# Qkv stage in steps of 256 rows, the first ones beside chunks 10 to 15 of the convolution

## The reference

```python
K = 2.0 * einsum('chn,hnl->chl', C_term, V).real        # 16 images, 256 channels, 64 states -> 256 positions
h = K
h = h + attn(_layernorm(h))    # layer_norm, qkv, elu(q)+1, elu(k)+1, kv = sum k v, ksum = sum k,
                               # (q kv) / (q ksum), proj, residual, layer_norm, fc1, gelu, fc2, residual
h = h + ffn(_layernorm(h))     # sigmoid(x Wq routers^T), 256 leaf probabilities, leaf values, Wout
```

## Time and profile before

| | us |
|---|---|
| median of 3 runs | 537.11 |
| the profiled execution | 535.44 |
| its span | 533.6 |
| PE busy in the span | 444.3 (83%) |
| DVE, ScalarE, GpSimd busy | 357.8, 286.7, 184.6 |
| chain of waits: PE, DVE, issue, ScalarE, GpSimd | 60%, 18%, 8%, 7%, 4% |

### The profile page before, as it was taken

The page is one execution under the profiler, slowest core; times in us unless marked ns, Lnnn a source line. Parts: engine busy times, 40 slices in busy tenths (PEclk is TensorE's granted clock), DMA queues, the critical chain, the costliest instruction groups (busy, mean ns, idle before and its releaser), DMA issues.

```text
span 533.6 us, 11354 instructions
## 1 busy us (share of the span) xinstructions
PE 444.3 (83%) x3724; PEld 401.4 (75%) x3724; DVE 357.8 (67%) x854; ACT 286.7 (54%) x592; POOL 184.6 (35%) x166
## 2 busy tenths in 40 slices
PE   0076666668999997799999999999999999998983
PEld 0066655556777776698998998998988988998973
DVE  5999999666778655254657567567566576485764
ACT  3814554457766673545754654555466366446621
POOL 0597998130211111051810811612504406306020
PEclk9997999899999999699999999999999999999988
DMA  4624657711111221000101101002002001001011
GB/s 120 209 86 110 162 157 222 211 54 72 41 41 59 102 67 41 25 16 0 41 2 40 40 0 58 20 0 79 0 0 79 0 0 39 0 0 39 1 41 39
DMA packets 37817, 30.86 MB, mean 58 GB/s; under 512 B 19488, under 2 KB 31136, under 8 KB 37792
## 3 DMA queue, kind: packets, MB, share of 16 engines
q1 hardware_dynamic: 18688, 22.04, 12.9%
q10 hardware_dynamic: 19104, 8.52, 5.6%
HBM read 17.97 MB, written 12.58 MB: 57 GB/s over the span
## 4 chain that ended last, share of the span: by engine, by line
PE 60%; DVE 18%; issue 8%; ACT 7%; POOL 4%; DVEq 1%; DMA 1%; ACTq 0%; SPq 0%; POOLq 0%
PE PS L297 17%; PE PS L299 16%; PE PS L298 16%; PE PS L1458 6%; DVE Mb L988 3%; PE PS L1587 3%; DVE M L991 3%; PE PS L1513 2%; DVE lTl L1193 1%; DVE outb L1253 1%; ACT PS L628 1%; DVE bst L1199 1%; ACT yh L632 1%; ACT kr L660 1%; ACT lTh L740 1%
## 5 line engine op out<-in xcount | busy, mean ns | idle before, releaser
L1222 DVE TENSOR_TENSOR gl<-PS,gh 128x512 fp32r<-128x512 f32 x56 | 38.7, 691 | 65.6 <-ACT gh L748 37.2
L745 ACT ACTIVATE PS<-PS,fc1bias 128x512 f32<-128x512 f32 x56 | 36.7, 656 | 76.6 <-PE PS L299 76.6
L297 PE MATMUL PS<-fc2h,gh 128*128 128x256 f32 x256 | 74.4, 291 | 2.4 <-DVE gl L1349 1.4
L299 PE MATMUL PS<-fc2l,gh 128*128 128x256 f32 x256 | 72.4, 283 | 0.0
L298 PE MATMUL PS<-fc2h,gl 128*128 128x256 f32 x256 | 72.3, 283 | 0.0
L489 POOL TENSOR_SCALAR pst<-mv 128x4 f32<-128x4 f32 x15 | 3.4, 228 | 181.7 <-DVE pst L1206 181.7
L297 PE MATMUL PS<-x2Th,fc1h 128*128 (+2 forms) x144 | 55.3, 384 | 2.1 <-DVE x2Tl L1193 2.1
L298 PE MATMUL PS<-x2Th,fc1l 128*128 (+2 forms) x144 | 53.7, 373 | 0.0
L299 PE MATMUL PS<-x2Tl,fc1h 128*128 (+2 forms) x144 | 53.3, 370 | 0.0
L297 PEld LDWEIGHTS PS<-fc2h,gh 128*128 128x128 f32 x256 | 48.7, 190 | 5.8 <-DVE pst L1206 1.6
L298 PEld LDWEIGHTS PS<-fc2h,gl 128*128 128x128 f32 x256 | 48.8, 191 | 1.2
(11 more groups left out here) (229 smaller groups left out, 1366.0 us busy)
## 6 DMA issues: line engine op xcount, KB each, us to landing
h_scratch<-tokev ACTq DMA_DIRECT2D x16, 256.0 KB, 3.1
h<-h_scratch SPq DMA_DIRECT2D x16, 256.0 KB, 4.9
q_scratch<-qe ACTq DMA_DIRECT2D x16, 256.0 KB, 2.1
qf<-q_scratch SPq DMA_DIRECT2D x16, 256.0 KB, 3.0
out_tokens<-outb SPq DMA_DIRECT2D x16, 256.0 KB, 2.1
craw<-in_c_ri SPq DMA_DIRECT2D x16, 128.0 KB, 2.6
craw<-in_c_ri SPq DMA_DIRECT2D x32, 64.0 KB, 2.3
fc1raw<-in_fc1T SPq DMA_DIRECT2D x1, 1024.0 KB, 6.2
```

Of the source, the lines that this page charges most:

```text
L297: pe.matmul(dst, ah, bh, start=start, stop=False, **kw)
L299: return pe.matmul(dst, ah, bl, start=False, stop=stop, **kw)
L745: act.activation(bank(j % 2), bank(j % 2), ACT.Gelu, bias=fc1bias[:, j:j + 1]).then_inc(gact, 1)
L1222: dve.tensor_tensor(gl[:, j % 2, :], bank(j % 2), gh[:, j % 2, :].bitcast(F32), ALU.subtract).then_inc(gldone, 1)
```

## The change

The qkv stage becomes 16 steps of 256 rows: step s is half `s // 8` of images 2(s mod 8) and 2(s mod 8)+1. As steps 0 to 7 need only the first half of `h0`, `scales`, `norm1`, q, k and v of steps 0 to 3 are made in the same rounds as chunks 12 to 15, and the preparation of step 0 and 1 in the rounds of chunks 10 and 11. In these rounds one PSUM bank (0) takes the tokens of all chunks and one (7) the table; PE's `tokens` waits for the copy of the chunk before. The k/v of steps 0 to 7 stay in SBUF (k in `kvm`, v in `vt0`). For images 0 to 7 the sums of both halves are made together in the second pass (4 matmuls); for images 8 to 15 the first half is summed and masked in steps 4 to 8 (`kv_sums_ahead`), the second half later into `kvx`, and GpSimd adds the two (`add_halves`, 8 times 128x272). SyncE's queue now also sends the token rows of chunks 10 to 15 and all of q. The set-up operations on projection, gate, leaf, fc1 and fc2 weights are moved between the steps 4 to 10. Attention of images 0 and 1 stands behind step 12, projection behind step 14.

The core of the diff (numbers of lines are not kept):

```diff
+STEPS = 2 * GROUPS
+FIRST = 12
+SINGLE = 10
+SPREAD = STEPS - 4
+AHEAD = GROUPS
...
+            load_h0(0)
+            load_h0(1)
+            load_h0(2)
+            load_c(FIRST // 2, FIRST % 2)
+            store_h0(SINGLE)
+            for n in range(SINGLE + 1, CHUNKS):
+                if n + 2 < CHUNKS:
+                    load_c((n + 2) // 2, (n + 2) % 2)
+                load_h0(n - SINGLE + 2)
+                if n > FIRST:
+                    store_q(n - FIRST - 1)
+                store_h0(n)
...
+            rotate(SINGLE // 2, 0)
+            for n in range(SINGLE, CHUNKS):
+                if n + 1 < CHUNKS:
+                    rotate((n + 1) // 2, (n + 1) % 2)
+                scales(n - FIRST + 2)
+            for s in range(CHUNKS - FIRST + 2, STEPS):
+                scales(s)
...
+            add_proj_bias(0)
+            for c in range(AHEAD, AHEAD + 4):
+                add_halves(c)
+            rstd(0, x2done, 11, mv2, pst2, xh2done, 4, v2done)
+            for c in range(AHEAD + 4, B):
+                add_halves(c)
...
+            for n in range(SINGLE, CHUNKS):
+                s = n - FIRST
+                if s + 1 >= 0:
+                    norm1_apply(s + 1)
+                products(n, 7)
+                if s >= 0:
+                    q_elu(s)
+                product_sums(n, n % 2)
+                norm1_stats(s + 2)
...
+                if s + 1 >= 0:
+                    y_low(s + 1)
+                if s >= 0:
+                    k_elu(s, 0)
+                    k_elu(s, 1)
+
+            def step(s):
+                if s + 1 < STEPS:
+                    norm1_apply(s + 1)
+                q_elu(s)
+                if s > GROUPS:
+                    kv_mask(image(s - 1, 0))
+                elif image(s - 1, 0) >= AHEAD:
+                    kv_mask_ahead(image(s - 1, 0))
+                if s + 1 < STEPS:
+                    y_low(s + 1)
+                k_elu(s, 0)
+                if s + 2 < STEPS:
+                    norm1_stats(s + 2)
...
+                k_elu(s, 1)
...
+            for n in range(SINGLE, CHUNKS):
+                s = n - FIRST
...
+                if s >= 0:
+                    q_products(s)
+                if s + 1 >= 0:
+                    y_transposes(s + 1)
+                if s >= 0:
+                    kv_products(s, 0)
+                    kv_products(s, 1)
+                pe.wait_ge(tokout, CREDIT + (n if n > SINGLE else n - 1))
+                tokens(n, n % 2, 0)
+
+            def step(s):
+                q_products(s)
...
+                if s + 1 < STEPS:
+                    y_transposes(s + 1)
+                kv_products(s, 0)
...
+                kv_products(s, 1)
```

More of the change, by code:

```diff
@@ L346, in _ @@
                 load_weight(dst[:, :, :], src)
-            for n in range(2, CHUNKS):
+            for n in range(2, FIRST):
                 load_c(n // 2, n % 2)
@@ L735, in high @@
+            step(GROUPS + 3)
             def high(dst, b, made, g, used, uses, done):
@@ L1096, in kv_mask, with tile @@
-            def kv_mask(u, i):
-                c = 2 * u + i
-                dve.wait_ge(ksmm, CREDIT + (3 + i if u == 0 else 2 * (c + 1)))
-                new = PS[:, 6 if u >= EARLY else 6 + i, 0:KD * (P + 1)].rearrange("p (k x) -> p k x", k=KD)
-                m = kvm[:, c, :, :]
+            for n in range(CHUNKS // 2, SINGLE):
+                products(n, 7 - n % 2)
+                product_sums(n, n % 2)
+            def tile(s, i):
+                return h0[:, s // GROUPS, image(s, i), :]
@@ L1159, in _ @@
+            step(CHUNKS - FIRST + 2)
+            step(CHUNKS - FIRST + 3)
+            dve.wait_ge(act_set, 5)
+            for j in range(2):
+                w = slice(j * JH // 2, (j + 1) * JH // 2)
+                tt(fc2l[:, w, :], fc2raw[:, w, :], fc2h[:, w, :].bitcast(F32), ALU.subtract)
+                step(GROUPS + j)
+            for k in range(KD):
+                dve.wait_ge(act_set, 6 + k)
                 link(dve.scalar_tensor_tensor(fc1l[:, k, :], fc1raw[:, k, :], nrm[:, 2, k:k + 1],
@@ L1494, in kv_products @@
[L1494 to L1500 removed]
+                        mm = three(pe, PS[:, 5, o * HT:(o + 1) * HT], qkvh[:, k, w], qkvl[:, k, w], yh[:, s % 2, k, :],
+                                   yl[:, s % 2, k, :], k == 0, k == KD - 1)
@@ L1512, in kv_sums, with kv_sums_ahead @@
+            def kv_sums_ahead(c):
+                pe.wait_ge(kdone, CREDIT + c + 1)
+                pe.wait_ge(kvact, CREDIT + 3 * (c + 1))
+                pe.wait_ge(kvdone0, CREDIT + 2 * (c - AHEAD))
                 for k in range(KD):
-                    mm = pe.matmul(PS[:, b, k * (P + 1):(k + 1) * (P + 1)], kt[:, p % 2, k * P:(k + 1) * P],
-                                   vt[:, p % 2, k, :], start=first and k == 0, stop=last, skip_group_check=True)
-                mm.then_inc(ksmm, 1)
+                    mm = pe.matmul(PS[:, 0, k * (P + 1):(k + 1) * (P + 1)], kvm[:, c, k, 0:P], vt0[:, c, k, :],
+                                   start=k == 0, stop=True, skip_group_check=True)
+                mm.then_inc(ksmm0, 1)
@@ L1579, in attention @@
+            step(CHUNKS - FIRST)
+            pe.wait_ge(tokout, CREDIT + CHUNKS)
+            for s in range(CHUNKS - FIRST + 1, SPREAD):
+                step(s)
             def attention(g, banks=(4, 5, 6)):
```

747 lines of the change are left out of this document (329 added, 418 removed).

## The result

| | us |
|---|---|
| kernel before, median of 7 runs | 536.95 (535.69 to 538.06) |
| changed kernel, median of 7 runs | 541.83 (540.01 to 542.54) |
| ratio | 1.0086, 95% interval 1.0068 to 1.0103 |
| predicted | 534.4, range 527 to 543 |

The change makes the kernel slower by 4.9 us, 0.9%. I had forecast 2.7 us faster (534.4 against 537.11); 541.83 lies inside the stated range, near its slow end. From the page of the changed kernel: busy time by engine, and the chain of waits by engine. Its span is 539.1 us.

The account below looks back on a forecast made before the run. DVE holds the convolution, mutual waits the qkv start, PE 122 to 204 us. Terms from 72.81 sum to 215.05, plus 1.0: first fc1 at 216.1, 2.7 earlier; 535.44 becomes 532.7, as median 534.4, range 527 to 543.

Parts of the forecast that it names:

- the circle: Steps 5 to 12: hand-overs from transposes to transposes take 7.0 us a step, PE waiting about a microsecond in each.
- the stop: Rounds of chunks 11, 13 and 14: GpSimd's `Wa` holds DVE's `mr`, which has two SBUF inputs, 0.7 us each.
- Terms 1 and 2: Rounds of chunks 10 and 11, 16.1 us to the first q matmul; then rounds of chunks 12 to 15, 30.9.
- Term 3: Steps 5 to 12: 57.9 us, eight steps of 7.0 plus 1.9 showing of 5 us of set-up operations.
- Term 4: Steps 13 and 14: 16.7 us, two of 7.2 and 2.3 for attention's DVE operations.
- term 5: Up to the first projection matmul: 4.95 us, `mr` or a k held once behind the bias operation and an addition of halves.
- Term 6: Projection to first fc1 matmul: 14.0 us instead of 17.33, the residual following its matmuls at once.
- Afterwards unchanged: From the first fc1 matmul to the end: carried over as long as before; another length would mean wrong altogether.
- B: Chunk rounds: `mr`, only 128x2 elements, is not held and stays at 0.16; -2.9 us, 531.5; chance 0.16.
- C: Chunk rounds: `mr` waits for both GpSimd products, 2.33 instead of 0.7, rounds near 9; +5.3 us, 539.7; chance 0.18.
- E: Steps: hand-overs of a nine-station loop are longer than the smallest, 7.4 a step; +5 us, 539.5; chance 0.20.
- D: Steps: the circle is shorter, PE sets the pace at about 6.0 a step; -8.8 us, 525.6; chance 0.06.

Follow-up runs that it names:

- e5: Changed kernel with DVE's set-up operations moved ahead of `yl`, and SyncE storing q of step 10 before its wait for the last set-up: 537.67 us, ratio 1.002.
- e1: Changed kernel with GpSimd's two operand products (`Wa`, `Wb`) waiting until DVE has made `xh` and `mr` of the same round: 534.56 us, ratio 0.996.
- b1: Kernel before with only three small tiles allocated earlier, moving `gh` and the tiles behind it by 192 bytes: 532.81 us, ratio 0.993.
- e2: Changed kernel with e1's wait, and `qe` moved behind the statistics in the rounds of chunks 12 to 15: 532.00 us, ratio 0.9919.
- e4: Changed kernel with only DVE's set-up operations moved within their step, from ahead of `xh` to ahead of `yl`: 540.37 us, ratio 1.0074.
- e6: Changed kernel with e2's edits, statistics behind the normalisation, e5's set-ups and store, and GpSimd's projection bias waiting for `xh` of step 15: 521.18 us, ratio 0.9713.

## Why the prediction was wrong

**What bounds what** was right: DVE in the rounds, the circle in the steps, not PE. The sign was not. Two steps of the prediction failed: the stop, which it put on `mr` at 0.7 in three rounds, and the set-ups, of which it let 3.1 of 5 us vanish in a wait of DVE. The same stop at step 15 comes on top, and the stretch behind fc1, taken as unchanged, was not.

**Terms 1 and 2, the stop.** The prediction let GpSimd's products stop `mr`, because it has two inputs in SBUF, 0.7 in three rounds. Measured: `xh` is stopped, by 2.3 to 2.5 us in each of four rounds, 9.7 in all against the 2.1 that I had. `mr` comes when `Wb` is just over (83.07 against 83.00 in the round of chunk 11), so it takes 0.14 and never meets a product. `xh` has one tile and two per-partition values as inputs, so by the rule that I used it was free. The Trainium skill's page "SBUF — State Buffer", section "Who interferes with whom", has a second rule in the same list: a `tensor_scalar` that enters a mode with two ports excludes GpSimd too. It lets an operation be held that the first rule leaves free, and the rows agree that `xh` is held (3.03 against 0.74). They don't show such a mode: alone, `xh` takes 0.41 for 256 columns, as long as the k operation with two tensor inputs (0.41 in the earlier trace rows). So that GpSimd's products hold `xh` is shown, and why is not. I had left that rule out.

Other errors hide in these two terms. The `h0` loads landed 3.5 us after their issue instead of 4.9, and DVE waited 0.27 for the first instead of 1.7. The scales of step 0 began 0.8 late, behind `Wb` of chunk 11, and those of step 1 were held by the remainder of the qkv weights (their first operation took 1.64 instead of 0.22), so that the first round of term 2 is 7.3 without the stop, not 6.4. And the 1.2 for matmuls at half clock cost nothing: behind q of step 0 the granted clock was 0.60 from 90.2 to 93 us, but DVE set the pace and waited 0.64 before `xh` in that round as in the next ones. Term 2 is then 30.9 + 6.0 + 0.9 - 1.2 = 36.6, measured 36.3.

**Term 3, the set-ups.** The circle itself I had at 7.0; e5 shows 7.25, nine stations at some 0.03 more, +2.0 in eight steps. Set-up operations I let show 1.9 of their 5 us. They showed 5.3, by the difference between the changed kernel and e5 (63.3 - 58.0), so +3.4. The step that failed is the half sentence that they stand where DVE waits for GpSimd: they do, but an operation with two inputs in SBUF stops GpSimd's power (1.89 instead of 1.03), so it lengthens the wait that I hid it in, and the gaps of PE that followed brought half clock. An estimate of the shares: if each of the eight steps is taken at the shorter of its two lengths in the changed kernel and in e1, they sum to 61.3, so that about 2.0 of the 5.3 are the lower clock and 3.3 the delays themselves.

**Term 4** was 2.1 too small, as much as `xh` is held there (step 15, 2.81 instead of 0.74, behind the bias addition). I had put that stop on `mr` or a k in term 5, which came out 1.2 smaller. **Term 6** was right within 0.7, and the allowance of 1.0 for hand-overs covered it.

**Afterwards unchanged**: false by 4.3 us, in favour of the change. It was never a term of the sum, since the same instructions run; the memory plan in the diff, which I took for bookkeeping, made them 1% faster (3.2 us by b1, the rest open). Up to the first fc1 matmul the change costs 9.9 us, twice what the medians show. Without these 4.3 us the time would have been about 546, outside the stated range; that 541.83 lies inside it is luck. The prediction had named both this and a clock below 0.9 between 120 and 200 us as signs of being wrong altogether, and both were seen (0.60 and 0.62 in the windows above).

**Rivals.** B's sign was seen (`mr` at 0.14), but its condition is false: 128x2 elements do not spare it. Where `mr` met a GpSimd operation, the addition of halves at 210.02, it took 0.71, and 0.71 to 0.72 in e1, e2, e4 and e5. C had the size of the loss (2.33 for two products), rounds near 9 (9.7 measured) and the place in the order (`Wa` released just ahead of a DVE operation), with the wrong operation and a wrong reason: GpSimd did not keep both its turns, DVE brought two operations and lost one turn with each. It gave 539.7. E had the right size for term 3 (+5), of which its mechanism, slower hand-overs, made 2.0. D was not seen, but is what the experiments reach once the circle is cut and the set-ups are moved.

## What to carry to other kernels

Where GpSimd and DVE are released by the same event, look at which of the two is on the path and let the other wait for it: one wait was worth 7.3 us here, and with one DVE operation moved 9.8. Work that is made early and in small pieces forms a circle of hand-overs; before counting stations, ask which of them can be made one step ahead (the statistics here, 7.7 us, some 1.7 of them because a bias addition came out of the way of `xh`), and keep set-up work out of the gap in which another engine works for this one. When a wait is added or a part made faster, read the queues again: e4's gain was eaten by a store behind an unrelated wait, and the wait of e6 before the bias cost 2.9.

## What the runs showed of the hardware that I had not expected

- A normalisation in float32 from SBUF to SBUF with one tensor input (`xh`, 128x256) is held by GpSimd operations with inputs in SBUF: 1.48 and 1.63 us for two operations of about 0.4. Products with one input in PSUM beside the same GpSimd operations keep their 1.1 us.
- Two engines in each other's way take turns by operation. So a DVE operation in two pieces, coming 0.23 us after `Wa` began, lost two turns, 2.3 us; `qe` of e1, in one piece and coming 0.23 us after `Wb` began, with no product behind that, lost 1.1. `xh` in one piece was not tried.
- 192 bytes of memory plan were worth 4.0 us in the kernel before (ratio 0.993), with fc2's matmuls 283 to 279 ns; the same shift of fc1's operands made its 512-column matmuls 1% slower and its 256-column ones 1% faster.
- In these steps the granted clock fell to the lower level behind waits of PE of 2.15 and 2.42 us in the changed kernel and of 1.94 in e1. It stayed at the upper level behind one of 2.17 in e1, through those up to 1.77 in e5, and behind the one of 2.98 before step 15 of the changed kernel, where e5 fell behind 2.97. So the length of one wait does not tell whether the clock falls, but where it fell, a step cost 1.6 us more (9.24 against 7.65).
